# Orders of the front of an expert layer: block 0's rows, a gate half, the third activation

## The reference

```python
x = x + xattn(layernorm(x), ctx, Wq, bq, Wk, bk, Wv, bv, Wo, bo)   # 8 batches, 256 channels, 512 positions, 16 heads
x = x + ffn(layernorm(x), rms_weight, router_w, w_gate, w_up, w_down, sw_gate, sw_up, sw_down)

def ffn(x):
    ht = rmsnorm(x).reshape(2048, 512)
    topv, topi = top_k(softmax(ht @ router_w), 2)            # 8 experts, 2 for each row
    topv = topv / sum(topv)
    moe = sum over the 2 experts of a row: topv * ((silu(ht @ w_gate[e]) * (ht @ w_up[e])) @ w_down[e])
    sh = (silu(ht @ sw_gate) * (ht @ sw_up)) @ sw_down       # the shared expert, 512 -> 256 -> 512
    return moe + sh
```

## Time and profile before

| | |
|---|---|
| median of 3 runs | 834.0 us (829.28 to 836.18) |
| the profiled execution | 831.6 us, its span 829.9 us |
| TensorE busy | 782.5 us (94%) |
| VectorE busy | 548.2 us (66%) |
| ScalarE busy | 419.4 us (51%) |
| GpSimd busy | 363.6 us (44%) |
| granted TensorE clock, mean | 0.989 |

### The profile page before, as it was taken

The page is one execution under the profiler, slowest core; times in us unless marked ns, Lnnn a source line. Parts: engine busy times, 40 slices in busy tenths (PEclk is TensorE's granted clock), DMA queues, the critical chain, the costliest instruction groups (busy, mean ns, idle before and its releaser), DMA issues. The chain is left out here.

```text
span 829.9 us, 11858 instructions
## 1 busy us (share of the span) xinstructions
PE 782.5 (94%) x3877; PEld 395.3 (48%) x3877; DVE 548.2 (66%) x1048; ACT 419.4 (51%) x800; POOL 363.6 (44%) x309
## 2 busy tenths in 40 slices
PE   7999999999999999999999999998989999999993
PEld 3434334434334343343333455775445666666662
DVE  5787888898888888878888767777643233322331
ACT  2115666767767777677776674310333233333331
POOL 4207427317328155182222421000127777777774
PEclk9999999999999999999999999999999999999997
DMA  8957476566565765667543235511925666666663
GB/s 282 217 116 195 98 161 144 111 133 154 136 139 120 169 153 111 146 133 152 131 83 121 93 104 216 216 51 38 360 70 97 98 100 102 100 94 99 98 100 44
DMA packets 54186, 109.67 MB, mean 132 GB/s; under 512 B 12200, under 2 KB 27304, under 8 KB 49888
## 3 DMA queue, kind: packets, MB, share of 16 engines
q1 hardware_dynamic: 37080, 79.39, 38.4%
q0 software_dynamic: 16960, 29.37, 19.0%
q10 hardware_dynamic: 88, 0.16, 0.1%
HBM read 67.90 MB, written 40.86 MB: 131 GB/s over the span
## 5 line engine op out<-in xcount | busy, mean ns | idle before, releaser
L1061 DVE TENSOR_REDUCE negmax<-front_ps 128x1 f32<-128x512 f32 x512 | 326.7, 685 | 69.2 <-PE front_ps L911 67.4
L811 ACT ACTIVATE probs<-st_ps 128x512 f32<-128x512 f32 x512 | 284.6, 598 | 151.8 <-PE st_ps L945 135.0
L1340 POOL DMA_INDIRECT out<-ring,row_i x78 | 122.5, 1571 | 66.5 <-ACT ring L1393 50.6
L1564 PE MATMUL big_ps<-w_gu,attn 128*128 x244 | 113.0, 601 | 3.5 <-ACT attn L1386 3.5
L648 POOL CAST early<-early 128x512 fp32r<-128x512 f32 x28 | 17.1, 610 | 165.9 <-ACT early L764 165.9
L1773 DVE TENSOR_TENSOR zeros<-attn,big_ps 128x256 f32<-128x256 f32 x39 | 16.4, 421 | 83.0 <-ACT attn L1405 83.0
L945 PE MATMUL st_ps<-stacks 50*128 50x512 f32 x256 | 68.5, 493 | 2.2 <-ACT probs L811 1.9
L1405 ACT ACTIVATE attn<-big_ps 128x256 f32<-128x256 f32 x39 | 15.0, 384 | 109.8 <-PE big_ps L1564 109.8
L1323 POOL DMA_INDIRECT ring<-h_rows,row_i x39 | 39.5, 1014 | 68.2 <-DMA out<-x_sb 56.6
L958 PE MATMUL pv_ps<-probs,v_t 128*32 128x512 f32 x512 | 68.2, 605 | 0.5 <-ACT probs L811 0.5
L958 PE MATMUL pv_ps<-probs,early 128*32 128x512 f32 x512 | 68.2, 605 | 0.3
(11 more groups left out here) (212 smaller groups left out, 1219.3 us busy)
## 6 DMA issues: line engine op xcount, KB each, us to landing
parts_dram<-early SPq DMA_DIRECT2D x32, 512.0 KB, 4.4
stacks<-parts_dram SPq DMA_DIRECT2D x32, 256.0 KB, 5.4
w_gu<-in_gate_up SPq DMA_DIRECT2D x8, 1024.0 KB, 12.7
x_sb<-in_x SPq DMA_DIRECT2D x8, 512.0 KB, 9.7
early<-in_ctx POOLq DMA_DIRECT2D x8, 512.0 KB, 5.5
stacks<-parts_dram SPq DMA_DIRECT2D x32, 128.0 KB, 6.1
k_stack<-parts_dram SPq DMA_DIRECT2D x16, 256.0 KB, 4.6
q_stack<-parts_dram SPq DMA_DIRECT2D x16, 256.0 KB, 5.3
```

What stands on the lines that cost most here:

```text
L811: nc.scalar.activation(probs[:, k % 2, u % GH, :], score_bank(UNITS * s + u), ACT.Exp, scale=SCALE).then_inc(exp_done, 1)
L1061: nc.vector.tensor_reduce(negmax[:, n % 2, c:c + 1], smax_bank(UNITS * n + u), AX_X, ALU.max, negate=True).then_inc(max_done, 1)
L1340: nc.gpsimd.indirect_dma_start(outs[i], bass.IndirectOffsetOnAxis(ap=row_i[:, k:k + 1], axis=0), y_sb[:, k % RING, DY * i:DY * (i + 1)], N ...
L1564: mm = nc.tensor.matmul(gu_ps[:, :], h_t[:, k % 2, a, :], w_gu[:, bass.ds(expert, 1), a, :], start=(a == 0), stop=(a == DT - 1))
```

## The change

- VectorE, attention: the row statistics come one step after the residual they follow (not in the last half), and in half 14 the steps of the scale of 12 row tiles are spread and lie two units later.
- TensorE, attention: the fourth filler of half 14 moves from unit 14 to unit 16, and two matmuls of zeros with 256 columns stand behind the last product with the values.
- ScalarE, front: the copy of block 0's turned rows (`turn_in(0)`) stands ahead of the high parts of experts 6 and 7.
- TensorE, front: logits of tiles 14 and 15 stand behind the second half of gate product 2; then down tiles 0 and 1, the first half of gate product 3, the counts, its second half, down tiles 2 and 3.
- VectorE, front: `shared_add(2)` and `shared_add(3)` stand behind the prefix sums, `shared_act(3)` behind the positions.

```diff
-        def row_variance(dve, lo, hi, scale=1.0, eps=LN_EPS):
+        def row_variance(dve, lo, hi, scale=1.0, eps=LN_EPS, first=None):
-            for t in range(lo, hi):
+            for t in range(lo if first is None else first, hi):
                 last = nc.vector.bn_aggr(mv[:, t, :], stats[:, t, :])
...
-                        if s == HALVES - 2 and u in (2, 6, 10, 14):
+                        if s == HALVES - 2 and u in (2, 6, 10, 16):
                             pe.wait_ge(x1_ready, X1_START + CT * outputs_before(s))
...
                 pv(STEPS * HALVES - 1)
+                for _ in range(2):
+                    nc.tensor.matmul(st_ps[:, 0, 0:F], zeros[:, 0:P], zeros[:, 0:F], start=True, stop=True)
...
                             residual(dve, out_batch(s - 1), 1, proj_ps[:, :])
+                        if u == 2 and spread(s - 1) and out_batch(s - 1) is not None:
                             row_stats_of(out_batch(s - 1), 1)
...
                             residual(dve, out_batch(s), ended_at(late_units(s), u), proj_ps[:, :])
-                            row_stats_of(out_batch(s), ended_at(late_units(s), u))
+                            if s == HALVES - 1:
+                                row_stats_of(out_batch(s), ended_at(late_units(s), u))
+                        if s < HALVES - 1 and out_batch(s) is not None and ended_at(late_units(s), u - 2) is not None:
+                            row_stats_of(out_batch(s), ended_at(late_units(s), u - 2))
                         if s == HALVES - 2 and u == 0:
...
-                            token_variance(dve, 0, EARLY)
+                            for t in range(EARLY // 2):
+                                nc.vector.bn_aggr(mv[:, t, :], stats[:, t, :])
                         if s == HALVES - 2 and u == 2:
+                            row_variance(dve, 0, EARLY, 1.0 + RMS_EPS, LN_EPS * RMS_EPS, EARLY // 2)
+                        if s == HALVES - 2 and u == 4:
                             rstd_guess(dve, 0, EARLY)
-                        if s == HALVES - 2 and u in (4, 6, 8):
-                            rstd_step(dve, 0, EARLY, (u - 4) // 2)
+                        if s == HALVES - 2 and u in (6, 8, 10):
+                            rstd_step(dve, 0, EARLY, (u - 6) // 2)
...
-                for e in range(E):
+                def down_high_part(e):
                     act.wait_ge(wdn_loaded[e], 16)
                     nc.scalar.activation(w_dn_high[:, e, :, :], w_dn[:, e, :, :], ACT.Copy).then_inc(wdn_high, 1)
+                for e in range(KEPT):
+                    down_high_part(e)
...
                 turn_in(0)
+                for e in range(KEPT, E):
+                    down_high_part(e)
                 act.wait_ge(base_first, 16 * YCUT * 2 * RING)
...
-                shared_gates(2, (0,))
-                for t in range(EARLY, NTILE):
-                    logits(pe, t)
-                shared_gates(2, (1,))
-                for t in range(GT):
-                    shared_down(t)
-
+                for i in range(CT):
+                    shared_gates(2, (i,))
+                    for t in range(EARLY + CT * i, EARLY + CT * (i + 1)):
+                        logits(pe, t)
+                shared_down(0)
+                shared_down(1)
+                shared_gates(3, (0,))
                 pe.wait_ge(chosen_ready, 1)
...
-                shared_gates(3)
+                shared_gates(3, (1,))
+                shared_down(2)
+                shared_down(3)
                 shared_gates(4)
...
                 rows_low(dve, 3, everything, DT + 3)
-                shared_add(2)
-                shared_add(3)
...
                 run = src
+                shared_add(2)
+                shared_add(3)
...
-                shared_act(3)
                 nb, na, spare = blk[:, 45, :], blk[:, 46, :], blk[:, 47, :]
...
                 chained(dve, V.tensor_tensor(POS, POS, cnt_ps[:, 0, :, :], ALU.add))
+                shared_act(3)
                 for c, m in enumerate((M1, M2)):
```

## The result

Twenty runs of each kernel: before 834.87 us median (829.28 to 841.52), changed 826.31 us (823.81 to 830.7). The ratio is 0.9897 with a 95% interval of 0.988 to 0.9913: 8.6 us faster. The time lies in the predicted range, 0.8 us under the forecast of 827.1 us; the gain was forecast as 6.9 us. The two profiled executions differ by less: 831.6 and 825.6 us, spans 829.9 and 823.8 us. One execution each of the kernel before, of e2 and of e5 was slow (2476, 1083 and 1927 us) and counts in no ratio and no mean.

What follows compares the result with a forecast made beforehand. TensorE is busy nearly throughout, so its waits were taken to matter. Attention 3.1 + block 0 4.6 - front order 0.6 - zeros 0.2 = 6.9 us off the 834.0 us median: 827.1 us, range 822.5 to 832.5.

Steps and rivals of the forecast that it cites:

- Block 0's rows: Block 0's gate product: starts 2.8 us earlier and takes 3.60 for 5.39 us, together 4.6 us gained.
- The rival with the lower clock at this product: Block 0's gate product: clock falls anyway, turn counting as quiet; 1.8 us lost, 828.9 us; chance 0.13.
- The front order: TensorE and VectorE before the finding product: add and activation on VectorE make everything 0.6 us later.
- TensorE's order: Front: same matmuls rearranged, counts come when they came before, 0 to 0.2 us for one more change of kind.
- The attention: Moved statistics, scale and filler gain 0.9 + 2.2 = 3.1 us, bounds 0 and 4.
- its first wait: Half 13: TensorE's first wait of 0.75 us for a maximum goes away.
- the second wait: Half 13, at 449 us: another 0.75 us wait for a maximum goes, its gain contained in half 14's 2.2 us.
- the split maxima: Half 14: VectorE gets to them 0.7 us earlier, from 462.10 to 461.4.
- the wait that was to stay: Half 14: TensorE's filler still waits for VectorE, one step later; through at about 462.5 instead of 464.69, 2.2 us.
- Halves 5, 7, 9 and 11: Attention, halves 3 to 11: a stretch of 0.18 us goes away five times, 0.9 us.
- a half-clock stretch disappears elsewhere as well: Rival at the finding product: a 3.2 us stretch at 0.50 goes, worth 1.6 us; 825.5 us, chance 0.15.
- The zeros: Two zero matmuls behind the attention: TensorE drains last by 0.2 us at the barrier; cost 0.2, bounds 0 and 0.9.

Runs made afterwards that it cites:

- e2: Changed kernel with block 0's rows copied behind all eight high parts again; 831.13 us, ratio 0.9938 to the kernel before.
- e5: Kernel before with only block 0's rows copied ahead of the last two high parts; 831.32 us, ratio 0.9949 to the kernel before.
- e6: Kernel before with four unused matmuls between block 0's turn and its gate product, the copy staying late; 833.24 us, ratio 0.9969 to the kernel before.
- e1: The changed kernel again, unaltered, as yardstick; 825.91 us, ratio 0.9884 to the kernel before.
- e3: Changed kernel with TensorE's and VectorE's front orders (logits, gate half, down tiles, shared adds, third activation) as before; 827.38 us, ratio 0.9896.
- e4: Changed kernel with the attention's statistics, scale of 12 tiles and fourth filler as before; 830.29 us, ratio 0.9926 to the kernel before.
- e7: Changed kernel without the two matmuls of zeros behind the attention; 827.15 us, ratio 0.9896 to the kernel before.
- e8: Changed kernel with shared_add(2) and shared_add(3) behind the third activation; 823.43 us, ratio 0.9863 to the kernel before.
- e9: Changed kernel with the four logits in one row again, between the halves of gate product 2; 828.25 us, ratio 0.9912 to the kernel before.
- e11: Changed kernel with both shared adds behind the third activation, half 3's scale of 8 row tiles six units earlier, and no zeros; 824.37 us, ratio 0.9866.
- e10: Kernel before with only the new front orders of TensorE and VectorE; 834.47 us, ratio 0.9984 to the kernel before.
- e12: The kernel before again, unaltered, for a second profiled execution; 837.5 us, ratio 1.0023 to the other runs of the same program.

## Why the prediction was right, and where it was not

**Block 0's rows: right in place and size.** 2.8 us of wait and 1.8 us of clock were forecast; the profiles show 2.76 (3.53 to 0.77) and 1.69 (5.39 to 3.70), e2 and e5 give 4.5 and 4.3 us in the runs, e6 the clock alone. The rival with the lower clock at this product did not come. It leaned on the Trainium skill, "TensorE: Matmul & The Clock Gate", Part 4, by which a transpose doesn't count as TensorE being busy in the same way as other matmuls. In all nine profiles in which the wait there was 0.77 us (the changed kernel, e1, e3, e4, e5, e7, e8, e9, e11) it took 3.69 or 3.70 us; in the four with 2.94 to 3.76 us of waiting (before, e2, e10, e12) it took 5.17 or 5.39. How the array counts a transpose stays open; a wait of 0.77 us behind one does no harm here.

**The front order: the step that failed.** I cost it at 0.6 us and wrote that TensorE's order was "the same matmuls in another order, 0 to 0.2 us for one more change of kind". In an execution without a half-clock stretch there the 0.6 us hold, and so does the reason for them, the add and the activation on VectorE: 64.86 against 64.37 us. But in five of the six profiles with four logits in one row (e3, e5, e6, e9, e12; not the first one of before) the clock fell between 530 and 540 us, and in none of the eight with two pairs (changed, e1, e2, e4, e7, e8, e10, e11). From barrier to finding product the five profiles with the old order took 64.37, 67.54, 65.93, 65.92 and 65.90 us (before, e3, e5, e6, e12), 65.9 on average, the new order 64.8 to 64.9. So by the profiles the new order gains about 1.1 us on average, where I had a loss of 0.6; the runs of e3 (1.0 us) and e10 (1.3 us) have the same sign, and neither excludes zero. That it is the splitting of the logits rests on e9, one profile beside those counts. Why a row of such matmuls is followed by it stays open.

**The attention: right in kind, 3.1 forecast, 2.4 measured.** Half 13 gave 0.61 us between its residuals (7.78 to 7.17), where its first wait was priced at 0.75: the wait is gone, but a pass for maxima two steps on takes 0.52 us instead of 0.40. From its last residual to the one at 493.8, which holds the second wait and the filler of half 14, 1.0 us went (46.77 to 45.77) and not 1.45 (2.2 less the first 0.75). Here a step of the forecast failed: VectorE did not get to the split maxima 0.7 us earlier. They end 14.97 us after the residual (463.02 - 448.05), before it was 14.90 (462.10 - 447.20). TensorE reaches the filler behind them all the same, and the wait that was to stay is gone, so the order of its own steps was the limit; one of these steps waits 0.45 us for ScalarE. TensorE's timeline of the changed kernel:

```profile
463.47 1.13 PE L837 MATMUL proj_ps<-zeros 128*128 128x512 f32 x2
```

Halves 5, 7, 9 and 11 gave 0.19 us each (7.09 to 6.90 between the first two residuals of half 5), as forecast. For half 3, the fifth of them, nothing is shown: in the eight profiles without a stretch there its residuals lie 7.25 to 7.67 us apart with the old attention (before, e4, e5, e6) and 7.12, 7.40, 7.98 and 8.11 us with the new (e2, e3, e8, e9). The sum is 0.61 + 1.0 + 0.76, 2.4 us. What may come on top is a stretch in half 13 that three of the six profiles with the old attention have (e6, e10, e12) and none of the eight with the new; that is suggestive, no more.

**What neither the forecast nor the experiments explain: the finding product.** TensorE waited 2.45 or 2.46 us ahead of it in twelve profiles. With the old attention the half-clock stretch followed in five of six (before, e4, e5, e6, e12; not e10), with the new attention in none of six (changed, e1, e2, e3, e7, e9), whatever the front order. I had this case among the rivals (a half-clock stretch disappears elsewhere as well, 825.5 us, a chance of 0.15) and put no term into the sum. The profile of the changed kernel shows it, and the measured 826.3 lies between this rival and the forecast. Why the attention should matter some 65 us later stays open; the pattern was seen afterwards, and no run was made to test it.

**The zeros:** 0.2 us forecast, 0.4 measured.

**The sum.** The terms as measured in the profiles are 4.5 + 2.4 - 0.5 - 0.4 = 6.0 us. The spans of the first two profiles differ by 6.1, and that they agree so well is partly luck: the span up to half 3 (0.95 us longer) and half 3 with its stretch (1.20 longer) nearly cancel the part from the finding product to block 0's turn (27.15 to 25.54, 1.61 shorter, without its stretch) and the blocks behind the first gate product and turn (0.75 shorter).

The runs say 8.6. The mean granted clock of the runs says where the rest is: (1 - clock) x span is the time given away, by an estimate that counts about 5 us at the end where TensorE has nothing left to do. 70 runs of before have a mean clock of 0.9853, 12.3 us; 20 runs of the changed kernel 0.9924, 6.3 us. So of 9.3 us between the means of these two sets 6.0 go with the clock and 3.3 with everything else. I had given the clock 1.8 us and the rest 5.1; the profiles' terms without the clock make 4.3. Between 4.3 and 3.3 lies what such an estimate cannot resolve, for one step in the last digit of a clock is 0.8 us.

By the counts in the profiles the 6.0 can be placed, again as an estimate: 1.7 us at block 0; at the logits 5 of 6 times 1.5 us (65.9 against 64.37), 1.3 us; at the finding product 5 of 6 times 1.6 us, 1.3 us; in half 13 3 of 6 times 1.5 us (9.28 us between the residuals in e6 against 7.78), 0.8 us; 5.1 us together. Only the first was in the forecast. The number came out near because a term too large (rest) and one too small (clock) partly cancelled, and so far it was luck.

## What to carry to other kernels

Before a profile is costed, its mean granted clock is to be compared with that of the other runs: here 0.989 against a mean of 0.985, and the stretches of some 1.5 us in half 13 and at the logits, which no profile of the changed attention and of the split logits has, were not in it. A wait of TensorE is priced as the wait plus the share of executions in which a half-clock stretch follows it, and that share needs more than one profile. A row of tiny matmuls (here 32 with 8 columns) belongs on the same list although TensorE counts as busy in it. Splitting it by real work was cheap here: the whole new front order cost 0.5 us in an execution without stretches, and that was VectorE's order. On an engine with an order of its own, an add that waits for a late partner belongs behind the work that doesn't (e8, 2.1 us in the profile).

## What the runs showed of the hardware

- The clock can fall to 0.50 without any idleness of TensorE that the trace shows: in e3 the busy share from 530 to 540 us is full, the row of 32 matmuls with 8 columns (529.31 to 534.04) and matmuls with 512 columns behind it, and the clock is 0.66 in the mean of both windows. This happened in five of six profiles with such a row. With two rows of 16 and a gate half between them it happened in none of eight.
- The same wait may or may not be followed by it. Before the finding product TensorE waited 2.45 or 2.46 us in twelve profiles; five of these products took 4.23 to 4.55 us (before, e4, e5, e6, e12), seven took 2.94 us (changed, e1, e2, e3, e7, e9, e10). A wait of 1.3 us in half 3 was followed by it in five of thirteen (changed, e1, e7, e10, e12). Waits of 2.94 to 3.76 us ahead of block 0's gate product, behind the turn, were followed by it in four of four (before, e2, e10, e12). The Trainium skill, "TensorE: Matmul & The Clock Gate", Part 1, says of the start of a kernel that the number of matmuls at the low clock varies from run to run; the profiles show such variation in the middle of a kernel.
- Waits of 0.77 us (nine profiles) and 1.12 us (at the barrier, seven profiles) were not followed by it.
- Matmuls whose result nobody uses, put into such a wait, kept the clock for the next product: in e6 it took 3.70 us instead of 5.39.
